# Two attention layers and two feed-forward layers: the order of three engines inside the attention steps

## The chip, the cores and the metric

The kernel runs on one core of a Trainium2 chip. The metric is the time of one execution on the device in microseconds (us). Three runs of the kernel before took 850.15, 852.05 and 856.15 us, so the median is 852.05 us.

The core's engines run side by side, each through its own list of instructions in order, and wait for each other at semaphores: TensorE (PE: matmuls and transposes), VectorE (DVE), ScalarE (ACT), GpSimd (POOL) and SyncE (SP), whose queue issues the transfers.

## The reference, cut to what matters

```python
x = x + xattn0(layernorm(x), ctx, mask, ...)     # x 4 x 1024 x 256, ctx 4 x 77 x 256, 16 heads of 16
x = x + experts(layernorm(x), ...)               # 6 experts, 2 chosen per row
x = x + xattn1(layernorm(x), ctx, ctx, ...)      # one key and one value head for all 16 query heads
x = x + ffn(layernorm(x), ...)                   # 256 -> 1024 -> 256, quantized piecewise-linear gelu

# either attention layer:
scores = einsum('bhnd,bhtd->bhnt', q, k) * scale (+ mask)
attn = softmax(scores, axis=-1)
out = einsum('bhnt,bhtd->bhnd', attn, v)         # then the output projection and the residual
```

The change is in the two attention layers. Everything is computed in float32 accuracy: an operand is split into a leading part and a rest, and three matmuls take the place of one.

## The kernel before, in words

The 4096 rows of x are cut into 8 blocks of 512. Each attention layer (0: steps G = 0 to 7, 1: steps G = 8 to 15) is a software pipeline with one step per block. In step G the kernel works on four blocks at once: scores and weighing of block G; queries and maxima of the next block n = G + 1; the output projection and residual of the one before, p = G - 1; the layer norm of block nm = G + 2. Names of the pieces, with their lines:

- `queries` (L141): 6 matmuls for each half c of the 256 query features, into bank W[c]. ScalarE copies the bank out as qh (`leading`), VectorE subtracts for ql (`rest`, L320 in layer 0, L323 in layer 1).
- `max_unit` (L377, in layer 0 also L380 with the mask): 16 units per block. Each multiplies 128 rows of qh by the keys of 4 heads into one of the two banks X, and VectorE's `take_maxima` (L333) reduces the bank to row maxima mx. Unit u waits until unit u - 2 has been reduced, since there are two banks.
- `turn_maxima` (L386): 4 transposes of mx, then a copy on ScalarE (L301), then a transfer from mt into the stacked query tile qst (L261). The maxima enter the scores as extra rows of the matmul's operand, so no score of the next step can start before this transfer has landed.
- `score` (L402, in layer 0 also L405 with the mask): 16 heads per step, three banks in turn; ScalarE's `exp` (L307) empties them into pt.
- `weigh` (L413): after 4 heads, a quarter, the values are weighed by the exponentials into bank U. Column 16 of each group of 32 holds the sum of the exponentials.
- `divide` (L341, L344, L346): VectorE transposes U into ut, takes the reciprocal of the sums and multiplies. `fold` (L352) transposes two finished quarters back. ScalarE (`lead_quotient`, L312) and GpSimd (`rest_quotient`, L283) make the parts oh and ol.
- `output` (L427, in layer 0 also L422 for the bias): waits for all oh and ol of block p, writes bank W[k]. `add` (L358) adds the bank to x. W[k] is then free for `norm.turn` (L127), which transposes the normed block nm; `norm.lead` and `norm.rest` (L132, L136) split it for the next step's queries.

The order on each engine is written out by hand in loops over G, with the heads i (TensorE) or h (ScalarE) as the clock: `if i in (5, 9, 13): att.weigh(...)` means that this quarter is weighed right after score i. VectorE has no such clock, its calls simply follow each other. The last quarter of block p is weighed at i = 1 of the next step.

In the texts below the layers' steps are told from one score 0 to the next score 0. Quarter 3 of p is `weigh(p, 3)`. "Units" are `max_unit`, "reductions" are L333.

## Time and profile before

| | |
|---|---|
| median of three runs | 852.05 us |
| the profiled execution | 849.2 us |
| its span | 847.4 us |
| busy TensorE / VectorE | 90% / 79% of the span |
| busy ScalarE / GpSimd | 62% / 45% |
| layer 0, score 0 of G = 1 to score 0 of G = 7 | 65.4 to 223.2 us |
| layer 1, score 0 of G = 9 to score 0 of G = 15 | 467.25 to 610.3 us |

The span is what the trace covers, the execution's own time is 1.8 us more. A busy share says how much of the span an engine had work in flight. A TensorE instruction is booked from its issue to its modelled end and overlaps the next one, so start-to-start distances tell what it costs. "Granted clock" is TensorE's clock as a share of 2.4 GHz. The experts (249 to 443 us) and the last feed-forward layer (628 us on) are untouched.

### The profile page before, as it was taken

The numbers are of one execution on the slowest core, as the hardware profiler recorded it, in microseconds if no ns is written. First come the engines' busy times: TensorE is split into PE (matmuls) and PEld (weight loads), VectorE is DVE, ScalarE is ACT, GpSimd is POOL, SyncE is SP. The second block draws the span as 40 slices with busy tenths as digits, with TensorE's granted clock in tenths as the row PEclk, the third lists the DMA queues.
The fourth block names the chain that finished last, engine by engine and source line by source line (L and its number), as shares of the span: only waits on it lengthen the run. The fifth ranks groups of instructions, "written<-read, shape, count | busy, mean of one in ns | idle before, by whom it ended". The sixth has DMA issues, their size and how long they took to land.

```text
span 847.4 us, 13594 instructions
## 1 busy us (share of the span) xinstructions
PE 758.7 (90%) x4388; PEld 556.8 (66%) x4388; DVE 671.9 (79%) x1590; ACT 521.9 (62%) x943; POOL 377.9 (45%) x309
## 2 busy tenths in 40 slices
PE   4799999999899999999989888899888999999995
PEld 3456566665458787877764544455456888889895
DVE  7657777777857777777786888887859899999885
ACT  3455555555644446554436576666667888888884
POOL 5533322223213434344413232122137888988985
PEclk9999999999999999999987999999999999999999
DMA  7965633455100000001066555644400000000001
GB/s 221 157 171 112 141 72 67 97 110 103 46 28 1 1 1 7 2 1 51 1 86 92 76 77 67 115 63 56 58 0 2 2 26 26 26 12 15 26 26 50
DMA packets 24957, 48.51 MB, mean 57 GB/s; under 512 B 3670, under 2 KB 6871, under 8 KB 24376
## 3 DMA queue, kind: packets, MB, share of 16 engines
q1 hardware_dynamic: 23366, 46.54, 28.7%
q10 hardware_dynamic: 1522, 1.11, 0.4%
q8 instruction: 36, 0.59, 0.3%
q14 instruction: 33, 0.27, 0.1%
HBM read 11.99 MB, written 4.19 MB: 19 GB/s over the span
## 4 chain that ended last, share of the span: by engine, by line
PE 54%; DVE 19%; POOL 8%; issue 7%; ACT 6%; DMA 6%; ACTq 0%; DVEq 0%; POOLq 0%
PE bank L141 15%; PE bank L402 6%; PE bank L377 5%; PE bank L427 5%; PE bank L635 5%; DMA qst<-mt 5%; PE bank L413 4%; DVE mx L333 4%; POOL eex L514 4%; PE bank L799 4%; PE bank L405 2%; DVE fpart L754 2%; PE bank L127 2%; POOL frise L706 2%; DVE x L603 2%
## 5 line engine op out<-in xcount | busy, mean ns | idle before, releaser
L307 ACT ACTIVATE pt<-bank 77x512 f32<-77x512 f32 x256 | 146.5, 589 | 122.8 <-PE bank L405 76.3
L333 DVE TENSOR_REDUCE mx<-bank 128x4 f32<-128x308 f32 x256 | 108.9, 471 | 30.5 <-PE bank L380 17.8
L402 PE MATMUL bank<-qst,l_kst 128*77 128x512 f32 (+1 forms) x256 | 107.5, 433 | 19.9 <-DMA qst<-mt 13.9
L706 POOL TENSOR_TENSOR frise<-fg,fg 128x512 f32<-128x512 f32 x64 | 99.2, 1550 | 13.4 <-ACT fg L724 8.9
L377 PE MATMUL bank<-l_kblk,qh 128*128 128x308 f32 x256 | 90.2, 370 | 11.6 <-DVE mx L333 9.4
L402 PEld LDWEIGHTS bank<-qst,l_kst 128*77 128x77 f32 (+1 forms) x256 | 37.0, 149 | 84.2 <-issue 47.9
L103 POOL TENSOR_TENSOR rstd<-var,minus_half 128x4 f32<-128x4 f32 x32 | 34.4, 1074 | 121.1 <-DVE var L98 67.4
L377 PEld LDWEIGHTS bank<-l_kblk,qh 128*128 128x128 f32 x256 | 50.0, 196 | 55.3 <-issue 45.9
L283 POOL TENSOR_TENSOR ol<-ot,oh 128x512 fp32r<-128x512 f32 x32 | 43.1, 1348 | 93.4 <-ACT oh L312 61.3
L603 DVE SCALAR_TENSOR_TENSOR x<-bank,eweight,x 128x256 f32<-128x256 f32 x192 | 79.5, 476 | 4.4 <-PE bank L635 4.1
L799 PE MATMUL bank<-fw2h,fyh 128*128 128x256 f32 x256 | 72.3, 282 | 3.8 <-DVE fyl L766 3.8
L114 ACT ACTIVATE xn<-x,shift,rstd 128x256 f32<-128x256 f32 (+1 forms) x128 | 67.4, 589 | 10.8 <-POOL shift L105 10.8
L713 POOL TENSOR_TENSOR fy<-fpart,fg 128x512 f32<-128x512 f32 x48 | 67.6, 1408 | 13.5 <-DVE fpart L754 10.2
L413 PE MATMUL bank<-pt,l_vall 128*32 128x512 f32 x512 | 69.4, 614 | 4.6 <-DVE ut L341 2.0
L799 PE MATMUL bank<-fw2l,fyh 128*128 128x256 f32 x256 | 72.1, 282 | 0.0
L799 PE MATMUL bank<-fw2h,fyl 128*128 128x256 f32 x256 | 71.9, 281 | 0.0
L754 DVE SCALAR_TENSOR_TENSOR fpart<-ffixed,frise 128x512 f32<-128x512 uint16 x64 | 61.8, 966 | 9.2 <-POOL frise L706 9.2
L635 PE MATMUL bank<-ew2h,ehh 128*128 128x256 f32 x192 | 56.6, 295 | 10.3 <-DVE x L603 10.3
L635 PE MATMUL bank<-ew2l,ehh 128*128 128x256 f32 x192 | 54.6, 285 | 0.0
L635 PE MATMUL bank<-ew2h,ehl 128*128 128x256 f32 x192 | 54.5, 284 | 0.0
L522 ACT ACTIVATE eh<-bank 128x512 f32<-128x512 f32 x48 | 28.7, 597 | 39.7 <-PE bank L141 38.6
L799 PEld LDWEIGHTS bank<-fw2h,fyh 128*128 128x128 f32 x256 | 48.3, 189 | 7.2 <-DVE fyl L766 4.8
(178 smaller groups left out, 2127.9 us busy)
## 6 DMA issues: line engine op xcount, KB each, us to landing
qst<-qh SPq DMA_DIRECT2D x64, 256.0 KB, 6.8
qst<-ql SPq DMA_DIRECT2D x32, 256.0 KB, 9.4
out<-x SPq DMA_DIRECT2D x8, 512.0 KB, 2.6
qst<-ml SPq DMA_DIRECT2D x8, 480.0 KB
x<-in_x SPq DMA_DIRECT2D x3, 1024.0 KB, 12.7
weights<-in_mlp_w SPq DMA_DIRECT2D x2, 1024.0 KB, 5.0
mraw<-in_mask SPq DMA_DIRECT2D x8, 154.0 KB
x<-in_x SPq DMA_DIRECT2D x2, 512.0 KB, 5.9
```

What stands on the lines that cost most here:

```text
L141: last = self.nc.tensor.matmul(out, w, a, start=(first and k == 0), stop=(k == len(ops) - 1))
L307: self.nc.scalar.activation(self.pt[0:T, i // 4 % 2, i % 4, :], self.bank_of(G, i)[0:T, :], ACT.Exp).then_inc(self.probs, 1)
L333: self.nc.vector.reduce_max(out, banks[u % len(banks)][:, 0:4 * T].rearrange("q (p par t) -> q p par t", p=2, par=2), AX.X).then_inc(self. ...
L377: last = self.nc.tensor.matmul(bank, self.qh[:, c, tile], keys, start=True, stop=not layer.masked)
L402: last = self.nc.tensor.matmul(out, layer.kst[rows, layer.stack(c * HC + 2 * k + par), b * T:(b + 1) * T], self.qst[rows, self.slot(G), c ...
L413: last = self.nc.tensor.matmul(self.U[32 * k:32 * k + 32, :], layer.vall[:, self.batch(G), layer.value(c * HC + 2 * k + par), :], self.pt[ ...
L603: last = self.nc.vector.scalar_tensor_tensor(tile, part, self.weight[:, g % 2, 2 * k + t, e:e + 1], tile, ALU.mult, ALU.add)
L635: last = self.nc.tensor.matmul(self.OUT[k][:, t * D:(t + 1) * D], a[:, e % self.R, tile], w[:, e, :], start=(j == 0), stop=(j == 2))
L706: self.nc.gpsimd.tensor_tensor(self.rise[:, k % 2, :], self.g1[:, k % self.R, :], self.g0[:, k % self.R, :], ALU.subtract).then_inc(self.r ...
L713: self.nc.gpsimd.tensor_tensor(self.y[:, k % 2, :], self.part[:, k % 2, :], self.g0[:, k % self.R, :], ALU.add).then_inc(self.y_ready[0], 1)
L754: self.nc.vector.scalar_tensor_tensor(self.part[:, k % 2, :], self.fractions[:, k % self.R, :, 0], 2.0 ** -16, self.rise[:, k % 2, :], ALU ...
L799: last = nc.tensor.matmul(self.OUT[2 * (g % 2) + t // 2][:, t % 2 * D:(t % 2 + 1) * D], a[:, k % self.R, t * P:(t + 1) * P], w[:, c, :], s ...
```

## The change

It does four things, all within the attention steps.

1. `divide` is taken apart. `unfold` (the transpose of U, still once per quarter) stands alone; the new `divide` takes the reciprocals and the quotients of two quarters in one instruction each (tile rden has 32 numbers per partition, not 16).
2. On VectorE the parts of block p's last quarter no longer stand in one run behind four reductions, but singly between pairs of reductions. In layer 1 the first two reductions come ahead of the second `rest`.
3. On TensorE units, queries, weighing and outputs are put at other heads. Both outputs now follow score 10.
4. On ScalarE `lead_quotient` of the first half comes one head earlier, and in layer 1 both `norm.lead` stand together after head 12.

The diff, cut to its core (of layer 0's VectorE loop, which is rearranged like layer 1's, only the different part is shown):

```diff
+    def unfold(self, dve, G, q):
+        dve.wait_ge(self.weighed, 4 * G + q + 1)
+        self.nc.vector.transpose(self.ut[:, q % 2, :], self.U[:, :]).then_inc(self.unfolded, 1)
+
+    def divide(self, dve, G, c):
         nc = self.nc
-        c, par = divmod(q, 2)
-        k = 4 * G + q
-        dve.wait_ge(self.weighed, k + 1)
-        nc.vector.transpose(self.ut[:, q % 2, :], self.U[:, :]).then_inc(self.unfolded, 1)
-        dve.wait_ge(self.unfolded, k + 1)
-        group = self.ut[:, q % 2, :].rearrange("p (j d) -> p j d", d=32)
-        nc.vector.reciprocal(self.rden[:, q % 2, :, :], group[:, :, DH:DH + 1]).then_inc(self.inverse_ready, 1)
-        dve.wait_ge(self.inverse_ready, k + 1)
-        nc.vector.tensor_tensor(self.o32[:, c, :, par, :], group[:, :, 0:DH],
-                                self.rden[:, q % 2, :, :].to_broadcast([P, N // 32, DH]), ALU.mult).then_inc(self.divided, 1)
+        dve.wait_ge(self.unfolded, 4 * G + 2 * c + 2)
+        group = self.ut[:].rearrange("p k (j d) -> p k j d", d=32)
+        nc.vector.reciprocal(self.rden[:], group[:, :, :, DH:DH + 1]).then_inc(self.inverse_ready, 1)
+        dve.wait_ge(self.inverse_ready, C * G + c + 1)
+        nc.vector.tensor_tensor(self.o32[:, c, :, :, :].rearrange("p j k d -> p k j d"), group[:, :, :, 0:DH],
+                                self.rden[:].to_broadcast([P, 2, N // 32, DH]), ALU.mult).then_inc(self.divided, 1)
...
+        UNITS1 = {1: (0,), 2: (1,), 3: (2,), 4: (3,), 5: (4, 5), 6: (6, 7), 7: (8, 9), 9: (10,), 10: (11,), 11: (14, 15)}
...
-                        if h == 3 and p >= BLOCKS:
+                        if h == 2 and p >= BLOCKS:
                             att.lead_quotient(act, p, 0)
...
@@ VectorE, layer 0 (outputs and units 12 to 15)
-                    if p >= 0:
-                        for k in range(2):
-                            att.add(dve, p, k)
+                    if p >= 0:
+                        att.add(dve, p, 0)
                     if n < BLOCKS:
                         att.take_maxima(dve, n, range(12, 16), att.X)
+                    if p >= 0:
+                        att.add(dve, p, 1)
...
@@ VectorE, layer 1
                     if n < 2 * BLOCKS:
-                        for c in range(C):
-                            att.rest(dve, n, c)
-                        att.take_maxima(dve, n, range(0, 4), att.X)
+                        att.rest(dve, n, 0)
+                        att.take_maxima(dve, n, range(0, 2), att.X)
+                        att.rest(dve, n, 1)
                     if p >= BLOCKS:
-                        att.divide(dve, p, 3)
+                        att.unfold(dve, p, 3)
+                    if n < 2 * BLOCKS:
+                        att.take_maxima(dve, n, range(2, 4), att.X)
+                    if p >= BLOCKS:
+                        att.divide(dve, p, 1)
+                    if n < 2 * BLOCKS:
+                        att.take_maxima(dve, n, range(4, 6), att.X)
+                    if p >= BLOCKS:
                         att.fold(dve, p, 1)
                     if n < 2 * BLOCKS:
-                        att.take_maxima(dve, n, range(4, 10), att.X)
-                    att.divide(dve, G, 0)
+                        att.take_maxima(dve, n, range(6, 10), att.X)
+                    att.unfold(dve, G, 0)
                     if n < 2 * BLOCKS:
-                        att.take_maxima(dve, n, range(10, 12), att.X)
+                        att.take_maxima(dve, n, range(10, 14), att.X)
                     if p >= BLOCKS:
-                        for k in range(2):
+                        for k in range(C):
                             att.add(dve, p, k)
                     if n < 2 * BLOCKS:
-                        att.take_maxima(dve, n, range(12, 16), att.X)
+                        att.take_maxima(dve, n, range(14, 16), att.X)
...
-                    att.divide(dve, G, 1)
+                    att.unfold(dve, G, 1)
+                    att.divide(dve, G, 0)
                     att.fold(dve, G, 0)
...
-                    att.divide(dve, G, 2)
+                    att.unfold(dve, G, 2)
...
@@ TensorE, layer 0
-                        if 3 <= i <= 10 and n < BLOCKS:
...
-                        if i in (5, 9, 13):
-                            att.weigh(pe, l0, G, i // 4 - 1)
...
+                        if i in (2, 4, 7, 9) and n < BLOCKS:
+                            for u in {2: (0, 1), 4: (2, 3), 7: (8, 9), 9: (10, 11)}[i]:
                                 att.max_unit(pe, l0, n, u, att.X)
+                        if i == 6:
...
+                                for u in (4, 5):
+                                    att.max_unit(pe, l0, n, u, att.X)
+                            att.weigh(pe, l0, G, 0)
+                            if n < BLOCKS:
+                                for u in (6, 7):
+                                    att.max_unit(pe, l0, n, u, att.X)
+                        if i == 10:
+                            for k in range(C):
...
+                                    att.output(pe, l0, p, k)
+                                if n < BLOCKS:
+                                    for u in (12 + 2 * k, 13 + 2 * k):
+                                        att.max_unit(pe, l0, n, u, att.X)
+                            att.weigh(pe, l0, G, 1)
+                        if i == 12:
+                            if n < BLOCKS:
+                                att.turn_maxima(pe, n, att.X[0])
+                            for c in range(C):
...
+                                    norm.turn(pe, nm, c, att.W[c])
+                        if i == 15:
+                            att.weigh(pe, l0, G, 2)
...
@@ TensorE, layer 1
-                        if i < C and n < 2 * BLOCKS:
-                            att.queries(pe, l1, n, i)
-                        if i == 1 and p >= BLOCKS:
+                        if i == 1 and n < 2 * BLOCKS:
+                            for c in range(C):
+                                att.queries(pe, l1, n, c)
+                        if i == 5:
+                            att.weigh(pe, l1, G, 0)
+                        if i in UNITS1 and n < 2 * BLOCKS:
+                            for u in UNITS1[i]:
+                                att.max_unit(pe, l1, n, u, att.X)
+                        if i == 2 and p >= BLOCKS:
                             att.weigh(pe, l1, p, 3)
...
+                        if i == 10:
+                            for k in range(C):
...
+                                    att.output(pe, l1, p, k)
+                                if k == 0 and n < 2 * BLOCKS:
+                                    for u in (12, 13):
+                                        att.max_unit(pe, l1, n, u, att.X)
+                        if i == 11:
+                            att.weigh(pe, l1, G, 1)
...
-                        if i in (11, 12) and nm <= LN_FFN:
+                        if i in (12, 13) and nm <= LN_FFN:
...
+                        if i == 14:
+                            att.weigh(pe, l1, G, 2)
```

How the instructions then stand, at three places of layer 1's step G = 11. First VectorE, from the rest of the queries to the additions of block p. Before:

```order
L323 TENSOR_TENSOR ql<-bank,qh 128x512 x2
L333 TENSOR_REDUCE mx<-bank 128x2x2 x4
L341 STREAM_TRANSPOSE ut<-bank 128x512
L344 RECIPROCAL rden<-ut 128x16
L346 TENSOR_TENSOR o_67<-ut,rden 128x16x16
L352 STREAM_TRANSPOSE ot<-o_67 128x512
L333 TENSOR_REDUCE mx<-bank 128x2x2 x6
L341 STREAM_TRANSPOSE ut<-bank 128x512
L344 RECIPROCAL rden<-ut 128x16
L346 TENSOR_TENSOR o_67<-ut,rden 128x16x16
L333 TENSOR_REDUCE mx<-bank 128x2x2 x2
L358 TENSOR_TENSOR x<-x,bank 128x512 x2
```

With the change:

```order
L323 TENSOR_TENSOR ql<-bank,qh 128x512
L333 TENSOR_REDUCE mx<-bank 128x2x2 x2
L323 TENSOR_TENSOR ql<-bank,qh 128x512
L338 STREAM_TRANSPOSE ut<-bank 128x512
L333 TENSOR_REDUCE mx<-bank 128x2x2 x2
L344 RECIPROCAL rden<-ut 128x32
L346 TENSOR_TENSOR o_67<-ut,rden 128x2x16x16
L333 TENSOR_REDUCE mx<-bank 128x2x2 x2
L352 STREAM_TRANSPOSE ot<-o_67 128x512
L333 TENSOR_REDUCE mx<-bank 128x2x2 x4
L338 STREAM_TRANSPOSE ut<-bank 128x512
L333 TENSOR_REDUCE mx<-bank 128x2x2 x4
```

The run of four VectorE instructions (L341 to L352) between reductions 4 and 5 is gone: one transpose (now L338), one joined reciprocal, one joined multiplication and the fold each have reductions around them, and reductions 12 and 13 stand ahead of the additions.

Second TensorE, from the quarter 3 of block p to the first score after `weigh(G, 0)`; L413 is `weigh`, L377 a unit. Before:

```order
L413 MATMUL bank<-pt,l_vall 32x512 x4
L402 MATMUL bank<-qst,l_kst 77x512 x2
L377 MATMUL bank<-l_kblk,qh 128x308 x2
L402 MATMUL bank<-qst,l_kst 77x512
L377 MATMUL bank<-l_kblk,qh 128x308 x2
L402 MATMUL bank<-qst,l_kst 77x512
L377 MATMUL bank<-l_kblk,qh 128x308 x2
L413 MATMUL bank<-pt,l_vall 32x512 x4
L402 MATMUL bank<-qst,l_kst 77x512
```

With the change:

```order
L377 MATMUL bank<-l_kblk,qh 128x308
L402 MATMUL bank<-qst,l_kst 77x512
L377 MATMUL bank<-l_kblk,qh 128x308
L413 MATMUL bank<-pt,l_vall 32x512 x4
L402 MATMUL bank<-qst,l_kst 77x512
L377 MATMUL bank<-l_kblk,qh 128x308
L402 MATMUL bank<-qst,l_kst 77x512
L377 MATMUL bank<-l_kblk,qh 128x308
L402 MATMUL bank<-qst,l_kst 77x512
L413 MATMUL bank<-pt,l_vall 32x512 x4
L377 MATMUL bank<-l_kblk,qh 128x308 x2
L402 MATMUL bank<-qst,l_kst 77x512
```

Unit 0 and unit 1 now stand ahead of `weigh(p, 3)`, and units are one per score up to unit 3.

Third TensorE, from `weigh(G, 1)` to the end of the step; L386 turns the maxima, L127 is `norm.turn`. Before:

```order
L413 MATMUL bank<-pt,l_vall 32x512 x4
L402 MATMUL bank<-qst,l_kst 77x512
L377 MATMUL bank<-l_kblk,qh 128x308 x2
L402 MATMUL bank<-qst,l_kst 77x512
L127 MATMUL bank<-ident,xn 128x128 x4
L402 MATMUL bank<-qst,l_kst 77x512
L386 MATMUL bank<-ident,mx 16x128 x4
L127 MATMUL bank<-ident,xn 128x128 x4
L402 MATMUL bank<-qst,l_kst 77x512
L413 MATMUL bank<-pt,l_vall 32x512 x4
L402 MATMUL bank<-qst,l_kst 77x512 x3
```

With the change:

```order
L377 MATMUL bank<-l_kblk,qh 128x308 x2
L413 MATMUL bank<-pt,l_vall 32x512 x4
L402 MATMUL bank<-qst,l_kst 77x512
L386 MATMUL bank<-ident,mx 16x128 x4
L127 MATMUL bank<-ident,xn 128x128 x4
L402 MATMUL bank<-qst,l_kst 77x512
L127 MATMUL bank<-ident,xn 128x128 x4
L402 MATMUL bank<-qst,l_kst 77x512
L413 MATMUL bank<-pt,l_vall 32x512 x4
L402 MATMUL bank<-qst,l_kst 77x512 x3
```

The first `norm.turn` has moved from ahead of the turned maxima to behind them, the last two units from behind `weigh(G, 1)` to ahead of it, and `weigh(G, 2)` by one score towards the step's end. In layer 0 the same transposes move in the same direction, and `weigh(G, 2)` is the last thing of the step.

## Rows read from the trace of the kernel before

**Rows 1.** Windows, one step each: us, busy us per engine (instructions), granted clock, DMA.

```profile
144.30:170.60 26.30, 25.32 (x146) 16.30 (x146) 19.69 (x48) 14.77 (x27) 7.13 (x8) 1.00 0.44 91
444.50:467.20 22.70, 19.61 (x80) 10.34 (x80) 15.56 (x41) 13.92 (x26) 6.90 (x5) 0.77 0.60 93
467.20:491.70 24.50, 22.07 (x112) 13.23 (x112) 19.94 (x48) 15.90 (x30) 5.07 (x5) 0.93 0.50 67
515.90:539.10 23.20, 20.83 (x113) 11.76 (x113) 19.29 (x50) 14.93 (x29) 5.12 (x5) 1.00 0.58 81
562.40:587.00 24.60, 22.08 (x112) 13.21 (x112) 20.06 (x48) 15.55 (x30) 6.41 (x7) 0.93 0.50 66
```

**Rows 2.** Chain of waits, a step of layer 0: start us, us, what.

```profile
144.32 0.46 PE bank L402
...
170.60 0.46 PE bank L402
```

**Rows 3.** Timeline of TensorE, same step: start us, us, instruction, idle before.

```profile
158.09 0.38 PE L377 MATMUL bank<-l_kblk,qh 128*128 128x308 f32 x1
...
164.69 0.31 PE L377 MATMUL bank<-l_kblk,qh 128*128 128x308 f32 x1
...
166.33 0.60 PE L386 MATMUL bank<-ident,mx 128*16 128x128 f32 x4
```

**Rows 4.** Chain of waits, a step of layer 1.

```profile
515.87 0.46 PE bank L402
516.33 1.39 PE bank L141 x6
...
519.34 0.99 PE bank L413 x8
...
528.51 1.44 PE bank L427 x12
...
536.14 2.90 DMA qst<-mt
...
539.08 0.46 PE bank L402
```

**Rows 5.** Timeline of TensorE, same step of layer 1.

```profile
520.79 0.45 PE L377 MATMUL bank<-l_kblk,qh 128*128 128x308 f32 x2
...
534.85 0.60 PE L386 MATMUL bank<-ident,mx 128*16 128x128 f32 x4
```

**Rows 6.** Timeline of VectorE, same step of layer 1.

```profile
516.33 1.40 DVE L90 BATCH_NORM_STATS2 stats<-x 128x6 f32<-128x256 f32 x4
...
520.00 0.69 DVE L323 TENSOR_TENSOR ql<-bank,qh 128x512 fp32r<-128x512 f32 x1 [0.92 <-ACT qh L296]
521.13 0.87 DVE L333 TENSOR_REDUCE mx<-bank 128x4 f32<-128x308 f32 x2 [0.44 <-PE bank L377]
...
524.44 0.71 DVE L352 STREAM_TRANSPOSE ot<-o 128x512 f32<-128x512 f32 x1
...
532.12 0.69 DVE L358 TENSOR_TENSOR x<-x,bank 128x512 f32<-128x512 f32 x1 [1.39 <-PE bank L427]
```

**Rows 7.** Instructions on tile rden, all steps: duration ns min/median/max, first and last start.

```profile
L344 DVE RECIPROCAL rden<-ut x64: 252/253/255, 55.6 to 629.9; 128x16 f32<-128x16 f32 x64
L346 DVE TENSOR_TENSOR o<-ut,rden x64: 424/425/1481, 55.9 to 630.1; 128x256 f32<-128x256 f32 x64
```

**Rows 8.** Groups of VectorE by form: busy us, mean ns, idle before us.

```profile
L136 DVE TENSOR_TENSOR xl<-bank,xh 128x512 fp32r<-128x512 f32 x32 | 21.5, 683 | 10.7 <-ACT xh L132 10.7
...
L584 DVE RECIPROCAL ertotal<-etotal 128x4 f32<-128x4 f32 x8 | 1.4, 178 | 0.3
```

**Rows 9.** Timeline of GpSimd, same step of layer 1.

```profile
525.95 1.28 POOL L283 TENSOR_TENSOR ol<-ot,oh 128x512 fp32r<-128x512 f32 x1 [2.19 <-issue]
```

**Rows 10.** Timeline of TensorE, last step of layer 0.

```profile
232.67 0.47 PE L422 MATMUL bank<-bias,ones 128*128 128x512 f32 x1 [2.76 <-POOL ol L283]
```

**Rows 11.** Timeline of GpSimd, end of a step of layer 0.

```profile
168.22 1.29 POOL L273 TENSOR_TENSOR ml<-mraw,mh 77x512 fp32r<-77x512 f32 x1
```

94 lines of the change are left out of this document (47 added, 47 removed).

## The prediction

> **What bounds the kernel now.** I read three views in this order. The windows, cut at the first score of a step, show that a step of layer 0 lasts 26.3 us with TensorE booked for 25.3 of them, and a step of layer 1 lasts 23.2 us with TensorE booked for 20.8 and VectorE for 19.3 [rows 1]. Neither engine is full in layer 1, so a chain through several must set its length. The chain of waits shows which: it comes back to the transfer of the turned maxima before each first score, 144.32 to 170.60 in layer 0 [rows 2] and 515.87 to 539.08 in layer 1, where the transfer alone takes 2.90 us [rows 4]. So a step has two pieces. From its score 0 to the turned maxima (TM) it takes 166.33 - 144.32 = 22.0 us in layer 0 [rows 2, 3] and 534.85 - 515.87 = 19.0 us in layer 1 [rows 4, 5]. From TM to the next score 0 it takes 4.3 us in layer 0 [rows 2, 3] and 4.2 in layer 1 [rows 4, 5]: transposes, copy, transfer. The change cannot shorten the second piece, only fill it. The timelines show what fills the first. In layer 0 it is TensorE, with stalls too small to be listed as idle: a unit's matmul that waits for its bank is booked at 0.38 us, a free one at 0.31 [rows 3]. In layer 1 it is a queue on VectorE: 16 reductions from 521.13 on, with the division, the fold and the additions between them [rows 6].
>
> **Layer 1, step by step.** First piece, until the first reduction. Before, it starts 5.26 us after score 0: both halves of the queries, `weigh(p, 3)` and two more scores are ahead of unit 0 on TensorE, and on VectorE the second `rest` at 520.00, itself 0.92 late, is ahead of the reduction [rows 6]. Afterwards unit 0 has ahead of it two scores (0.53 us, estimated from the 0.46 of the first and the spacing behind it) and two halves of 1.39 [rows 4], so it starts at 3.3; it reached its reduction 0.34 after its start (520.79 to 521.13 [rows 5, 6]), 0.44 with the first fill. The first reduction then starts at 3.75, **1.5 us earlier**.
>
> Second, from the first reduction to TM. VectorE's items now: 16 reductions of 0.435 (a pair books 0.87 [rows 6]), 7.0; `rest` 0.62; two transposes at 0.71 [rows 6], 1.4; one joined division; fold 0.7; two additions, 1.3. The joined division has no row. The multiplication of 256 numbers takes 0.425 [rows 7], one of 512 by the nearest row 0.683 [rows 8]. The reciprocal takes 0.178 for 4 numbers [rows 8] and 0.253 for 16 [rows 7], so by the same slope 0.35 for 32. Together 1.05 with gaps, where two single ones cost 1.4: **0.35 us saved per pair**, bounded by 0 and 0.68 (nothing gained, or one of the two free); I take the nearest rows. The items sum to 12.1 us. I add 0.8 for a unit's way there and back (one each time VectorE catches up with TensorE). The piece ends 12.9 us behind the first reduction; before it was 534.85 - 521.13 = 13.7. **0.8 us less.** What makes it shorter though it holds more: before, VectorE stood 1.39 us for the second output ahead of its last four reductions [rows 6], and TensorE stood while VectorE ran four instructions in a row.
>
> Third, TensorE has two `norm.turn` behind TM (four transposes are booked 0.60 [rows 3], 0.44 without the overlap of some 0.16), three scores of 0.24 and a weighing of 0.99 [rows 4]: 2.6 us of work in 4.2, hidden. VectorE has behind its last reduction an unfold, joined division, fold, two `norm.rest` and an unfold, in all 4.4 us, and then the statistics, 2.1 us from their row to the next `rest` [rows 6]; that `rest` can't start before qh is there, some 2.7 us into the step, so about 0.5 us of slack are left. The step is then 20.9 us, 2.3 less. I take 2.0, since the walk has no queueing noise in it; bounds are 0.4 (only the division's saving arrives) and 2.6 (the 0.8 vanish too). Six full steps, G = 9 to 14: **12.0 us** (2.4 to 15.6).
>
> The Trainium skill (VectorE: DVE Perf Modes, "The TRN2 errata") gives an SBUF-to-SBUF instruction a fixed part of 58 cycles, 0.06 us. By it a joined division would save 0.12 us and not 0.35, and six steps 1.4 us less. The trace disagrees: a reciprocal of 4 numbers takes 0.178 us [rows 8], so the fixed part is over twice that.
>
> **TensorE's clock.** Of the steps of layer 1, one at full granted clock (2.4 GHz) lasts 23.2 us, two at 0.93 last 24.5 and 24.6 [rows 1]. Part of such a step runs at 1.2 GHz, for 1.2 to 1.4 us. With less waiting per step I count one of the two gone: **1.2 us** (2.4 more lost to 2.4 gained).
>
> **First step of layer 1, G = 8.** It has no block p, lasts 22.7 us and has the lowest clock, 0.77 [rows 1]. Units and reductions are denser here too, and no unit waits for an output. I take **2.2 us**, as in a full step; bounds 0 and 4.0, the latter if the low clock goes as well.
>
> **Layer 0.** TensorE's own work up to TM: 13 scores with mask, 0.23 for each of two matmuls, 6.1; queries 2.8; three weighings of 0.99 with gaps of some 0.17, 3.5; 16 units of two matmuls, each booked 0.31 [rows 3] less the overlap of 0.16, 4.8; two outputs of 1.44 [rows 4] with a bias of 0.23, 3.3; one `norm.turn` 0.44. That is 20.9 of the 22.0 us, so 1.1 are stalls. The `norm.turn` moves behind TM: 0.44 gone for certain. Of the stalls the new spacing (two units per one or two scores, the division between pairs) removes some; I take half of the 1.1, so **1.0 us** a step, bounds 0.44 and 1.55. Seven steps, G = 0 to 6: **7.0 us** (3.1 to 10.9).
>
> **The last steps.** In G = 7 output 0 stood 2.76 us for GpSimd [rows 10]. Two more scores, 0.9 us, now stand ahead of it and fill that; behind, the weighings wait less for the exponentials. **1.3 us** (0 to 2). But `weigh(7, 2)` and `weigh(7, 3)` now stand back to back with an unfold of 0.71 between, which is counted in. In G = 15 two scores likewise, against a joined division on the way to the last output: **0.3 us** (-0.5 to 0.8).
>
> **Sum.** 12.0 + 1.2 + 2.2 + 7.0 + 1.3 + 0.3 = 24.0 us. The profiled execution took 849.2 us and would take 825.2. The median shown is 852.05, 2.85 above it, so I forecast **828.0 us** for the median. All low bounds together leave a gain of 2.6, all high ones 35.7.
>
> **Rivals.**
> - *The wait for the outputs comes back at another place.* In layer 1 the last two reductions stand behind both additions. The outputs now follow score 10, with the parts of p made later: fold, oh, ol. Before, ol ended at 525.95 + 1.28 = 527.2 [rows 9], 1.1 us before output 0 began; in my walk it ends 0.15 before. If VectorE's 1.4 us before the addition [rows 6] returns, six steps lose 8.4 and layer 0 half of its 7.0: 828 + 8.4 + 3.5 = 840 us. For it: that thin margin. Against it: TensorE gets to the outputs with units ahead that VectorE must have served.
> - *The clock falls in every step of layer 1.* The lowest granted clock stands in the step without outputs [rows 1], where units alternate with waits; the new order spreads units further. Six falls for two at 1.3 us: 828 + 1.2 + 5.2 = 834 us.
>  The Trainium skill (TensorE: Matmul & The Clock Gate, "HAM oscillation") has short idle stretches between groups of matmuls take the clock down and up again; by it each new gap costs, and the time would be these 834 us.
> - *GpSimd holds the division up.* The multiplication reads and writes SBUF only; its longest of 64 took 1.48 us where 0.425 is the median [rows 7]. In layer 0 the joined one stands just where GpSimd does mask instructions without a pause between, 1.29 us for one of them [rows 11]. Held until two have ended, with 1 us of slack: 1.6 us in seven steps, 11 us: 839 us.
>  The Trainium skill (SBUF — State Buffer, "Who interferes with whom") makes this an exclusive lock for the whole instruction when VectorE has two SBUF inputs; by it the wait is whole and not shared.
> - *Slower.* The chain fold, oh, ol, output, addition decides each step: output 0 comes late by more than 2.3 us in layer 1 and 1.4 in layer 0, because exponentials behind a late oh on ScalarE hold back scores and so TensorE. Each us beyond that costs 13 steps 13 us; 1 us gives 865. Against it: ol took 1.28 us [rows 9], and three banks let two scores run ahead of ScalarE.
> - *The joined instructions don't save.* The division's rows bound this at 4 us: 832.
>
> **Chances.** Forecast with its sizes (816 to 837) 0.66; wait comes back 0.14; clock 0.07; GpSimd 0.04; joined instructions 0.04; slower 0.05. The range for 8 in 10 goes from 817 to 843. A change under 1% (8.5 us) can't be told from none by a measurement of this kernel. Of the cases, the first rival half lands within 1%, as does a little of the forecast: faster 0.84, within 1% 0.11, slower 0.05.
>
> **What would show it.** Score 0 to score 0: about 25.3 us in layer 0 and 21.2 in layer 1. First reduction of layer 1 about 3.8 us after score 0. VectorE's wait before L358 nearly gone. L346 32 times at 0.69, L344 at 0.35. First score's wait for the transfer under 1 us in layer 0, still 1 to 1.5 in layer 1. Wrong, if VectorE waits before the additions or TensorE before the outputs in full steps, if L346 means over 0.9, or if the clock in layer 1's windows is below 0.93 in most.

## The result, and the profile after

The changed kernel takes **816.17 us** (median of four runs, 810.88 to 822.52) against 851.1 for the kernel before (four runs, 847.85 to 856.15). The ratio is 0.960, 95% interval 0.955 to 0.965: 4% faster. The forecast was 828.0 with a range of 817 to 843; the median lies 0.8 us under its lower end. The profiled execution took 817.71 us with a span of 815.9, 31.5 less than the 847.4 of before. The terms are compared against these 31.5 us; the medians lie 34.9 us apart, since the profiled execution of before is 1.9 us under its median and this one 1.5 over.

First the windows, one step each, to set beside [rows 1]: length, busy time (instructions) of TensorE's matmuls, its weight loads, VectorE, ScalarE and GpSimd, granted clock, DMA share, GB/s. The first is a step of layer 0, the second is G = 8, the others are two steps of layer 1.

```profile
139.91:164.71 24.80, 24.30 (x146) 16.50 (x146) 18.74 (x44) 14.33 (x27) 7.32 (x8) 1.00 0.48 97
...
431.59:449.78 18.19, 16.22 (x80) 8.49 (x81) 15.43 (x39) 14.24 (x26) 6.91 (x5) 1.00 0.74 113
...
511.35:531.96 20.61, 19.07 (x112) 11.61 (x112) 19.06 (x46) 14.90 (x29) 5.27 (x6) 1.00 0.69 118
531.96:552.49 20.53, 18.95 (x113) 11.71 (x113) 18.10 (x45) 15.09 (x30) 6.43 (x7) 1.00 0.60 80
```

A step of layer 0 went from 26.3 to 24.8 us, one of layer 1 from 23.2 to 24.6 down to 20.5, and G = 8 from 22.7 at a clock of 0.77 to 18.2 at 1.00. Next the chain of waits in the step of layer 1 from 511.35 on (start, us, what), beside [rows 4].

```profile
511.39 0.69 PE bank L402 x2
512.08 2.88 PE bank L141 x12
...
515.14 0.86 DVE mx L333 x2
...
519.85 0.62 DVE ot L352
...
522.78 1.57 PE bank L427 x12
...
524.64 1.42 PE bank L427 x12
...
529.09 2.87 DMA qst<-mt
531.96 0.04 issue
532.00 0.68 PE bank L402 x2
```

The first half of the step now belongs to VectorE, the second to TensorE with its two outputs. The timeline of VectorE in the same step, beside [rows 6]; the bracket is idle time before the row and what ended it.

```profile
515.14 0.86 DVE L333 TENSOR_REDUCE mx<-bank 128x4 f32<-128x308 f32 x2
515.92 0.68 DVE L323 TENSOR_TENSOR ql<-bank,qh 128x512 fp32r<-128x512 f32 x1
...
524.54 0.86 DVE L333 TENSOR_REDUCE mx<-bank 128x4 f32<-128x308 f32 x2 [0.91 <-PE bank L377]
525.32 1.47 DVE L358 TENSOR_TENSOR x<-x,bank 128x512 f32<-128x512 f32 x2
```

The 1.39 us ahead of the second addition are gone; 0.91 us now stand ahead of reductions 12 and 13. The first reduction starts at 515.14, where before it came 5.26 us into the step. TensorE's first output and the turned maxima of this step, and GpSimd's ol that the output needs, beside [rows 5, 9]:

```profile
522.70 0.35 PE L427 MATMUL bank<-l_woh,oh 128*128 128x256 f32 x1
...
527.79 0.60 PE L386 MATMUL bank<-ident,mx 128*16 128x128 f32 x4
```

```profile
521.26 1.29 POOL L283 TENSOR_TENSOR ol<-ot,oh 128x512 fp32r<-128x512 f32 x1 [3.25 <-issue]
```

ol ends at 522.55, the output begins at 522.70. The two instructions on tile rden in all steps (ns min/median/max, first and last start), beside [rows 7]:

```profile
L344 DVE RECIPROCAL rden<-ut x32: 330/353/355, 60.0 to 591.8; 128x32 f32<-128x32 f32 x32
L346 DVE TENSOR_TENSOR o<-ut,rden x32: 691/692/694, 60.4 to 592.2; 128x512 f32<-128x512 f32 x32
```

Where the 31.5 us came from, by score 0 of each step:

| stretch | forecast | measured |
|---|---|---|
| layer 0 up to score 0 of G = 7 | 7.0 | 8.9 |
| G = 7 and the experts | 1.3 | 4.1 |
| G = 8 | 2.2 | 4.5 |
| six steps G = 9 to 14, at full clock | 12.0 | 17.8 |
| the clock in these six | 1.2 | 2.1 |
| G = 15 and the last feed-forward layer | 0.3 | -5.9 |

For the fourth and fifth row: before, the six steps took 24.51, 24.11, 23.21, 23.43, 24.55 and 23.26 us. The first and the fifth hold a fall of the clock (0.93). The other four ran at 1.00 and mean 23.50, and 6 x (23.50 - 20.53) = 17.8; what the two had above 23.50, 2.1, is put down to the clock. The second, 24.11, is long for another reason: one multiplication of its division took 1.29 us where 0.425 is the median, and it stands on the chain of waits. GpSimd was at work when it began (the kernel before):

```profile
504.52 1.32 POOL L1075 TENSOR_TENSOR fw1l<-weights,fw1h 128x512 fp32r<-128x512 f32 x1 [1.40 <-ACT fw1h L1229]
```

```profile
504.83 1.29 DVE L346 TENSOR_TENSOR o<-ut,rden 128x256 f32<-128x256 f32 x1
```

The last row is a loss that nobody forecast. In the last feed-forward layer, whose code is unchanged, the clock fell four times. Windows of 2 us of the changed kernel around one of them:

```profile
670.00:672.00 2.00, 0.26 (x3) 0.05 (x1) 2.00 (x3) 1.97 (x5) 1.84 (x3) 1.00 0.20 80
672.00:674.00 2.00, 1.90 (x9) 1.65 (x10) 1.05 (x2) 1.97 (x5) 1.92 (x2) 0.84 0.45 182
674.00:676.00 2.00, 2.00 (x10) 1.83 (x9) 1.26 (x2) 1.40 (x3) 1.92 (x2) 0.50 0.00 0
676.00:678.00 2.00, 2.00 (x11) 1.84 (x11) 2.00 (x4) 1.14 (x3) 1.32 (x2) 0.81 0.00 0
```

TensorE idled from 670 to 672, worked again, and then ran at 0.50 (1.2 GHz) through a whole window: 0.16 x 2 + 0.50 x 2 + 0.19 x 2 = 1.7 us lost. The gap is a wait for ScalarE's normalized rows; the kernel before has it too, and no fall behind it. One row from the timeline of the changed kernel, then one from that of before, then two windows of before around it:

```profile
672.10 0.66 PE L127 MATMUL bank<-ident,xn 128*128 128x128 f32 x4 [1.85 <-ACT xn L114]
```

```profile
709.77 0.66 PE L127 MATMUL bank<-ident,xn 128*128 128x128 f32 x4 [1.88 <-ACT xn L114]
```

```profile
708.00:710.00 2.00, 0.23 (x2) 0.23 (x3) 2.00 (x3) 1.97 (x5) 1.92 (x2) 1.00 0.36 147
710.00:712.00 2.00, 2.00 (x13) 1.75 (x12) 0.86 (x3) 1.97 (x5) 1.92 (x2) 1.00 0.29 115
```

### The profile page after: what moved, and what is told of

Its sections match the earlier page's. It is cut to its first block, busy times and chain, and to the rows that moved or that the text cites. A ratio compares the mean times of both kernels' runs of the same rounds, so it can differ in the third digit from the quotient of the medians.

```text
span 815.9 us, 13530 instructions
## 1 busy us (share of the span) xinstructions
PE 739.3 (91%) x4388; PEld 556.8 (68%) x4388; DVE 655.0 (80%) x1526; ACT 515.4 (63%) x943; POOL 376.7 (46%) x309
## 3 DMA queue, kind: packets, MB, share of 16 engines
q1 hardware_dynamic: 23366, 46.54, 29.7%
## 4 chain that ended last, share of the span: by engine, by line
PE 52%; DVE 19%; POOL 8%; issue 7%; ACT 6%; DMA 6%; DVEq 0%; ACTq 0%; POOLq 0%
PE bank L141 16%; PE bank L635 6%; PE bank L427 5%; PE bank L402 5%; DMA qst<-mt 5%; PE bank L377 4%; PE bank L413 4%; POOL eex L514 4%; DVE mx L333 3%; PE bank L405 3%; PE bank L799 3%; DVE fpart L754 2%; POOL frise L706 2%; PE bank L380 2%; DVE x L603 2%
## 5 line engine op out<-in xcount | busy, mean ns | idle before, releaser
L307 ACT ACTIVATE pt<-bank 77x512 f32<-77x512 f32 x256 | 140.6, 588 | 85.3 <-PE bank L405 62.7
L333 DVE TENSOR_REDUCE mx<-bank 128x4 f32<-128x308 f32 x256 | 108.9, 470 | 24.4 <-PE bank L380 13.7
L402 PE MATMUL bank<-qst,l_kst 128*77 128x512 f32 (+1 forms) x256 | 103.0, 417 | 16.4 <-DMA qst<-mt 10.7
L706 POOL TENSOR_TENSOR frise<-fg,fg 128x512 f32<-128x512 f32 x64 | 97.0, 1516 | 18.4 <-ACT fg L724 13.9
L377 PE MATMUL bank<-l_kblk,qh 128*128 128x308 f32 x256 | 81.5, 336 | 9.8 <-DVE mx L333 6.0
L283 POOL TENSOR_TENSOR ol<-ot,oh 128x512 fp32r<-128x512 f32 x32 | 41.3, 1292 | 97.2 <-ACT oh L312 53.7
L402 PEld LDWEIGHTS bank<-qst,l_kst 128*77 128x77 f32 (+1 forms) x256 | 36.6, 146 | 65.7 <-ACT pt L307 24.8
L799 PE MATMUL bank<-fw2h,fyh 128*128 128x256 f32 x256 | 74.1, 289 | 3.8 <-DVE fyl L766 3.8
L377 PEld LDWEIGHTS bank<-l_kblk,qh 128*128 128x128 f32 x256 | 48.0, 192 | 43.2 <-issue 34.0
L413 PE MATMUL bank<-pt,l_vall 128*32 128x512 f32 x512 | 68.2, 604 | 2.0 <-ACT pt L307 1.0
L799 PEld LDWEIGHTS bank<-fw2h,fyh 128*128 128x128 f32 x256 | 50.3, 196 | 7.4 <-DVE fyl L766 4.8
L748 DVE TENSOR_SCALAR ffixed<-bank 128x512 int32<-128x512 f32 x64 | 43.5, 680 | 13.9 <-PE bank L141 13.6
```

Of the source, the lines that this page charges most:

```text
L307: self.nc.scalar.activation(self.pt[0:T, i // 4 % 2, i % 4, :], self.bank_of(G, i)[0:T, :], ACT.Exp).then_inc(self.probs, 1)
L333: self.nc.vector.reduce_max(out, banks[u % len(banks)][:, 0:4 * T].rearrange("q (p par t) -> q p par t", p=2, par=2), AX.X).then_inc(self. ...
L377: last = self.nc.tensor.matmul(bank, self.qh[:, c, tile], keys, start=True, stop=not layer.masked)
L402: last = self.nc.tensor.matmul(out, layer.kst[rows, layer.stack(c * HC + 2 * k + par), b * T:(b + 1) * T], self.qst[rows, self.slot(G), c ...
L413: last = self.nc.tensor.matmul(self.U[32 * k:32 * k + 32, :], layer.vall[:, self.batch(G), layer.value(c * HC + 2 * k + par), :], self.pt[ ...
L706: self.nc.gpsimd.tensor_tensor(self.rise[:, k % 2, :], self.g1[:, k % self.R, :], self.g0[:, k % self.R, :], ALU.subtract).then_inc(self.r ...
```

## The experiments

**The same kernel again.** No edit: are the four falls the change's?

> The changed kernel once more, nothing edited. It tells how far one profile can be trusted. First theory: the first 573 us repeat (a step of layer 0 24.8 us, of layer 1 20.5), and the 6 us that the changed kernel lost behind the attention layers, where the granted clock stood at 0.94 in four stretches of 30 us, do not belong to the change: the falls come and go from run to run. Then this profile shows another number of falls in the last feed-forward layer, and the time varies by up to 6 us with it. Rival: the falls come from where that layer now starts behind the shortened steps; then there are four again. Time expected: 810 to 822 us.

817.2 us (812.43 to 820.93, four runs; ratio 0.963, 0.960 to 0.966), span 810.6. The steps are the same: 24.8 us in layer 0, 20.5 in layer 1. In the last feed-forward layer, TensorE's waits and one of the windows (the three behind it, up to 768 us, also show 1.00):

```profile
PE bank L127 <- ACT xn L114: 10.3, 6, 1.9
```

```profile
648.00:678.00 30.00, 28.15 (x180) 25.27 (x180) 27.86 (x50) 26.93 (x49) 25.99 (x20) 1.00 0.08 32
```

The same six gaps, one of 1.2 us and five of 1.8 to 1.9, and no fall behind them. One fall stands just ahead of this layer, at 596 to 600 us, behind a wait of 1.88 us for ol; the first profile has that wait too, without a fall. So the falls vary from run to run of one kernel. The times go with the mean clock: the four runs took 812.43, 816.69, 817.72 and 820.93 us at mean granted clocks of 0.986, 0.982, 0.980 and 0.976. At equal clock the change keeps its gain, though its size is not sharp: before took 846.72 and 847.65 us at 0.986, 34 to 35 us above 812.43; 849.34 at 0.980, 32 above 817.72; 849.67 and 851.67 at 0.976, 29 to 31 above 820.93.

**The gap closed.** In the last feed-forward layer the turn of the next rows comes one part later on TensorE, ScalarE and VectorE:

```diff
-                    if c in (4 if g == 0 else 2, 6) and g + 1 < BLOCKS:
+                    if c in (4 if g == 0 else 3, 6) and g + 1 < BLOCKS:
...
-                    if c in (5 if g == 0 else 3, 7) and g + 1 < BLOCKS:
+                    if c in (5 if g == 0 else 4, 7) and g + 1 < BLOCKS:
...
-                    if c == (3 if g == 0 else 1) and g + 1 < BLOCKS:
+                    if c == (3 if g == 0 else 2) and g + 1 < BLOCKS:
```

> The changed kernel with one more edit: in the last feed-forward layer the first transposes of the next block, its copy and its rest each come one part later (part 2, 3, 4, not 1, 2, 3). There TensorE stood 1.85 us for ScalarE's normed rows, five times, and behind four of these gaps the clock fell. First theory: the gap is what lets the clock fall; without it there are no falls in that layer, and the gaps themselves are gone if nothing else limits: up to 5 x 1.85 = 9 us and 6 us of clock, 801 to 812 us. Rival: that layer is bound by GpSimd, VectorE and ScalarE together (each 83 to 97% busy), so TensorE's gap only moves to another place: then the time stays at 810 to 818 us, with falls or without.

810.73 us (810.66 to 811.07), ratio 0.954 (0.953 to 0.956), faster than both kernels. TensorE's waits in the same stretch:

```profile
PE bank L799 <- DVE fyl L766: 3.4, 3, 1.7
PE bank L127 <- ACT xn L114: 2.4, 5, 0.6
PE bank L141 <- DVE fxl L136: 2.4, 5, 1.0
```

8 us of waiting are gone, 5 came in at other places. The four runs lie within 0.4 us of each other, at the best value of the changed kernel (810.88, at a clock of 0.988). So closing the gap made the good case hardly shorter, and the four falls of the first profile are not there. One other fall is, of 1.7 us at 606 to 612, behind a wait of 2.70 us at the layer's start that both profiles of the changed kernel have without one. That the closed gap keeps the falls away is not shown: the four kernels below that stand on this one spread by 1.9 to 5.3 us over their runs.

**Only VectorE's order and the joined division** (TensorE and ScalarE as before):

> VectorE's order and the joined divisions of the changed kernel, TensorE's and ScalarE's order of the kernel before. Theory: in layer 1 a step is a queue on VectorE that TensorE has to feed in time; with TensorE's old order unit 0 still stands behind both queries, weigh(p, 3) and two scores, so the first reduction still starts 5.2 us after score 0, and only part of the 0.8 us behind it is won: 0.3 to 1.0 us a step in layer 1, 0 to 0.5 in layer 0, 843 to 849 us for a kernel before of 851. Rival: taking the division apart is the change's whole worth, TensorE's order follows from it: then 820 to 828 us.

845.77 us (840.73 to 853.32, ten runs), ratio 0.996 (0.992 to 1.000). Steps of 25.9 us in layer 0 and 23.65 in layer 1; three of the six of layer 1 hold a fall of the clock, the others took 22.94, 23.00 and 23.43. VectorE now waits for TensorE: its waits for units in layer 1, 470 to 570 us, and in layer 0, 65 to 225 us (us, times, longest), and a row of its timeline:

```profile
DVE mx L333 <- PE bank L377: 19.9, 19, 2.1
```

```profile
DVE mx L333 <- PE bank L380: 26.6, 24, 3.0
```

```profile
508.90 0.87 DVE L333 TENSOR_REDUCE mx<-bank 128x4 f32<-128x308 f32 x2 [2.05 <-PE bank L377]
```

In the kernel before these two sums are 5.2 and 13.7 us. VectorE is ready for the first maxima 2 us before TensorE delivers a unit. Its clock was also low: a mean of 0.958 to 0.984 in the ten runs.

**Only TensorE's and ScalarE's order** (VectorE as before, single divisions):

> TensorE's and ScalarE's order of the changed kernel, VectorE's order and single divisions of the kernel before. Theory: unit 0 comes 1.6 us earlier in layer 1, but VectorE takes it only behind the second rest (about 4.8 us after score 0 and not 3.8), then stands for the second output ahead of four reductions as before, which now comes later (behind score 10): 0 to 1.5 us a step won in layer 1. In layer 0 the transposes behind the turned maxima give 0.4 us a step, and the rest of the 1.5 us is lost: the kernel takes 832 to 848 us, and with dve_order_only the two parts do not add up to the 35 us of the whole. Rival: TensorE's order alone is worth most of it: 820 to 828 us.

851.88 us (849.55 to 856.33, ten runs), ratio 1.003 (1.000 to 1.005). My expectation of a gain was wrong. Steps of 27.2 us in layer 0, longer than the 26.3 of before, and 23.7 in layer 1. Here TensorE waits: in layer 0 from 65 to 225 us, then in layer 1 from 470 to 570.

```profile
PE bank L377 <- DVE mx L333: 12.1, 12, 1.3
```

```profile
PE bank L377 <- DVE mx L333: 6.9, 10, 1.0
PE bank L413 <- DVE ut L341: 4.2, 4, 1.1
```

The first was 1.0 us before. TensorE sends units between the outputs, where VectorE still stands for the output ahead of its last four reductions; two full banks later TensorE stands as well. So the halves of the change are worth 5 us less and 1 us more by themselves, and 34 together.

**The change with single divisions:**

```diff
-        nc.vector.reciprocal(self.rden[:], group[:, :, :, DH:DH + 1])...
+        for par in range(2):
...
+            nc.vector.reciprocal(self.rden[:, par, :, :], group[:, :, DH:DH + 1])...
+            dve.wait_ge(self.inverse_ready, k + 1)
+            nc.vector.tensor_tensor(self.o32[:, c, :, par, :], group[:, :, 0:DH], ...
```

> The change with the joined division taken back: at the place of each joined reciprocal and multiplication stand two single ones (16 reciprocals and 256 products each), everything else as in the changed kernel. Theory (VectorE's first pair lies on the way to the turned maxima in layer 1, layer 0 is TensorE's): single ones cost 2 x (0.25 + 0.425) against 0.35 + 0.69, so about 0.35 us more per pair; seven steps of layer 1 lose 0.35 each, layer 0 nothing: +2 to +3 us against the changed kernel, some 818 to 820 us. Rival 1 (the saving is absorbed where VectorE waits 0.9 us for units between the outputs): no difference, 816 to 817. Rival 2 (it counts in both layers and for both pairs): +5 to +10 us, 822 and more.

819.86 us (817.33 to 822.47), ratio 0.962 (0.957 to 0.967). The interval overlaps that of the change, so the trace has to tell: a step of layer 0 is 24.92 us against 24.78, and one of layer 1 (from one copy of the turned maxima to the next) took 22.05 in G = 9, with a fall of the clock at 460 to 464, and 20.72 on average in the five behind it, against 20.53.

```profile
L346 DVE RECIPROCAL rden<-ut x64: 209/244/252, 59.2 to 594.7; 128x16 f32<-128x16 f32 x64
L348 DVE TENSOR_TENSOR o<-ut,rden x64: 424/425/428, 59.4 to 595.0; 128x256 f32<-128x256 f32 x64
```

By 6 x 0.19 + 7 x 0.14 the joined division brings 2.1 us here (an estimate from these steps); 0.19 per step of layer 1 is about half of the 0.35 forecast for one pair. The forecast time, 818 to 820, was met, but more than 1 us of it is the fall.

**The joined division alone** in the old order, where the second quarter's division stood:

> The kernel before with one thing of the change: the divisions of two quarters joined, at the places where the second quarter's division stood before; orders of TensorE and ScalarE as before, and VectorE's otherwise too. Theory (the joined division is worth its 0.35 us where VectorE sets the turned maxima, layer 1 alone): 2 to 3 us less than before, ratio 0.997. Rival (it carries a large part of the change's gain of 34 us): ratio under 0.985. Rival (a longer block of VectorE between units costs what it saves): ratio 1.000 or over.

852.11 us (847.13 to 856.29, ten runs), ratio 1.002 (0.998 to 1.006): nothing. Layer 1's steps stay at 23.87 us on average (two hold a fall, as before), layer 0's grow from 26.3 to 26.7. One step did get shorter, G = 10, from 24.11 to 23.40: its product is not held here. In layer 0 the run transpose, division, fold lasts 2.5 us without a reduction in it, and VectorE's waits for the outputs rose from 13.3 us to this (layer 0):

```profile
DVE x L358 <- PE bank L427: 17.9, 12, 2.0
```

**Both turns behind the turned maxima, alone:**

```diff
-                        if i in (11, 12) and nm <= BLOCKS:
...
-                            norm.turn(pe, nm, i - 11, att.W[i - 11])
+                        if i == 12 and nm <= BLOCKS:
+                            for c in range(C):
...
+                                norm.turn(pe, nm, c, att.W[c])
```

> The kernel before with one thing of the change: both turns of the normalized block stand behind the turned maxima on TensorE in both layers (one stood ahead), with ScalarE's copies after them. Theory: in layer 0, where TensorE is the piece's bound, 0.44 us per step come off, 3 us in seven steps; in layer 1 the queue on VectorE sets the turned maxima and nothing comes off: ratio 0.9965. Rival (both layers): 6 us, ratio 0.993. Rival (the turns come late for the next step's queries): no gain or a loss, ratio 1.000 or over.

843.38 us (841.63 to 846.72), ratio 0.990 (0.985 to 0.995), more than expected. Layer 0's steps are 25.9 us, 0.4 less: the expected 0.44. Layer 1's are 23.4, all at full clock; the four that ran at full clock before too mean 23.3 against 23.5. At equal clock it is 4 us faster (842.45 at 0.984, where before took 845.96 and 847.38). The rest came with fewer clock falls: none between 444 and 600 us, where the profile of before has four windows of 12 us at 0.73 to 0.90. Whether the order keeps them away is open; its own runs went from 0.978 to 0.988.

**Both rests first**, on the kernel with the gap closed (810.73):

```diff
-                        att.rest(dve, n, 0)
-                        att.take_maxima(dve, n, range(0, 2), att.X)
-                        att.rest(dve, n, 1)
+                        for c in range(C):
+                            att.rest(dve, n, c)
+                        att.take_maxima(dve, n, range(0, 2), att.X)
```

> The changed kernel with the later turn in the second layer's feed-forward part (810.7 us), and in layer 1 both halves of the low query part (the rest) ahead of the first two reductions on VectorE, as before the change, instead of two reductions between them. Theory (VectorE's queue sets the first half of a step of layer 1): the first reduction starts 1.1 us later, after the second copy of qh, but the third only 0.5 later, and 0.4 to 0.5 us of it reach the step: 20.5 becomes 21.0 us, seven steps 3 us, 813.7 us. Rival (TensorE alone sets the step, with VectorE's 0.9 us of waiting for the units between the outputs as cover): 20.5 and 810.7. Rival (the whole 1.1 us reaches the step): 21.6 and 818.

813.95 us (813.78 to 815.69), ratio 0.957 (0.955 to 0.959); a step of layer 1 is 20.9 us. VectorE's timeline:

```profile
518.70 0.69 DVE L323 TENSOR_TENSOR ql<-bank,qh 128x512 fp32r<-128x512 f32 x1 [0.54 <-ACT qh L296]
519.31 0.85 DVE L333 TENSOR_REDUCE mx<-bank 128x4 f32<-128x308 f32 x2
```

The forecast 813.7 holds: the two reductions between the rests fill the wait for the second half of qh, and are worth 3.2 us. In the first half of such a step VectorE is the bound, as the forecast of this run had it.

**Units 14 and 15 ahead of output 1**, same base (VectorE takes their maxima ahead of both additions):

```diff
-        UNITS1 = {..., 9: (10,), 10: (11,), 11: (14, 15)}
+        UNITS1 = {..., 9: (10,), 10: (11,)}
...
-                                    for u in (12, 13):
+                                    for u in (12, 13, 14, 15):
...
-                        att.take_maxima(dve, n, range(10, 14), att.X)
+                        att.take_maxima(dve, n, range(10, 16), att.X)
```

> The same base (810.7 us). In layer 1 TensorE does units 14 and 15 behind 12 and 13, between the two outputs, instead of behind score 11, and VectorE takes their maxima ahead of both additions. Theory: in the changed kernel the end of the step's first piece is output 1, addition 1 (it can only start when output 1 ends), the last two reductions, turned maxima: 525.9 + 0.25 + 0.65 + 0.86 = 527.8 us in the step that began at 511.35. Without the addition on the way TensorE gets to the turned maxima when its own queue does, some 0.4 us earlier: 20.5 becomes 20.1 us, seven steps 3 us, 808 us. Rival (VectorE has only 1.1 us idle in a step, its queue behind the turned maxima sets the next step's first reduction): no gain, 810.7. Rival (additions late for the next norm): slower, 812 and more.

817.94 us (816.63 to 820.04), ratio 0.962 (0.959 to 0.964): 7 us slower than the base; a step of layer 1 takes 21.6 us. **The turned maxima also ahead of the second weighing:**

```diff
-                        if i == 11:
-                            att.weigh(pe, l1, G, 1)
-                        if i == 12 and n < 2 * BLOCKS:
-                            att.turn_maxima(pe, n, att.X[0])
+                        if i == 11:
+                            if n < 2 * BLOCKS:
+                                att.turn_maxima(pe, n, att.X[0])
+                            att.weigh(pe, l1, G, 1)
```

> As the run with units 14 and 15 between the outputs, and the turned maxima ahead of the second weighing on TensorE (0.99 us) instead of behind it, with ScalarE's copy of them behind exponential 11. Theory: up to 1.4 us less to the turned maxima; but VectorE has 19.4 us of work in a step of 20.5 and becomes the bound: 19.6 us a step, seven steps 6 us, 804.5 us. Rival (the transfer of 2.9 us then ends before TensorE's work behind the turned maxima is done, so the step falls only by TensorE's 0.9 us of waiting and its 0.65 for reductions): 19.2 to 19.6. Rival (ScalarE's exponentials hold it): no gain over the run without it.

816.02 us (813.08 to 818.41), ratio 0.958 (0.954 to 0.961); steps of 21.0 us, and 21.9 in the one with a fall of the clock. Both times my theory fell. TensorE's timeline in the second of them, then VectorE's:

```profile
528.17 0.77 PE L377 MATMUL bank<-l_kblk,qh 128*128 128x308 f32 x2 [0.52 <-DVE mx L333]
```

```profile
530.40 0.69 DVE L358 TENSOR_TENSOR x<-x,bank 128x512 f32<-128x512 f32 x1 [0.35 <-PE bank L427]
532.09 0.72 DVE L338 STREAM_TRANSPOSE ut<-bank 128x512 f32<-128x512 f32 x1 [1.01 <-PE bank L413]
```

TensorE stands 0.52 us for a bank between the outputs, which delays output 1 and all behind it, and VectorE stands 1.01 us for the weighing that moved back. Behind that transpose are the division, the fold, two rests and the statistics, which VectorE must finish before the next step's first reduction. With only some 1 us of idle time in a step it can't make up for 1.4 us of standing. Moving the turned maxima forward moved the wait onto the engine that had no room.

**The third weighing of layer 0's last step behind score 13**, same base. In the changed kernel TensorE stands there for a transpose:

```profile
234.02 1.06 PE L413 MATMUL bank<-pt,l_vall 128*32 128x512 f32 x8 [0.93 <-DVE ut L338]
```

```diff
-                        if i == 15:
+                        if i == (15 if n < BLOCKS else 13):
```

> The changed kernel with the later turn of the second layer's feed-forward part (which measured 810.7 us), and in the last step of layer 0's attention the third weighing behind score 13 instead of 15, so that the third and fourth don't stand back to back with VectorE's transpose of 0.7 between (a wait of 0.93 us before the fourth in the changed kernel). Theory: that wait goes, 0.9 us less: 809.8 us. Rival: the wait is only moved, since the last exponentials set the fourth weighing: 810.7 as without it.

812.47 us (811.75 to 814.15), ratio 0.953 (0.949 to 0.957): no gain, rather a loss. The last weighing begins 20.4 us after score 0 of this step, where it was 19.7. The wait is only moved, and there are two of them:

```profile
230.41 1.07 PE L413 MATMUL bank<-pt,l_vall 128*32 128x512 f32 x8 [0.73 <-ACT pt L307]
...
234.61 1.06 PE L413 MATMUL bank<-pt,l_vall 128*32 128x512 f32 x8 [0.68 <-ACT pt L307]
```

Both weighings now wait for exponentials.

## Why the prediction was right, and where its sizes were off

**The mechanism.** The forecast said that the chain through VectorE's queue and the outputs sets the steps of layer 1 and TensorE's own queue those of layer 0, and that interleaving shortens both. It did. What it did not say is that neither engine's order does it alone. The two one-sided kernels show this: 0.996 and 1.003.

**Layer 1, the walk.** Its three pieces came out nearly to the tenth. First reduction after score 0: forecast 3.75, measured 515.14 - 511.39 = 3.75. From there to the turned maxima: 12.9, measured 527.79 - 515.14 = 12.65. From there to score 0: 4.2, measured 532.00 - 527.79 = 4.2. The walk gave 2.3 us for this step, G = 11, and 23.21 - 20.61 = 2.6 was measured; over the four steps at full clock the gain is 3.0. The sizing step that failed is "I take 2.0, since the walk has no queueing noise in it". The new order has less waiting than the old (VectorE's waits from 470 to 570 us fell from 15.0 to 9.2), so the discount took 0.3 us off a number that was already 0.3 low. The walk also took G = 11, the shortest of the six steps, for all of them: G = 10 holds the multiplication of 1.29 us, 0.87 over the median, which the forecast knew from its row [rows 7] only as a risk for the new kernel and not as a cost of the old. Six steps brought 17.8 us, over the upper bound of 15.6.

**The joined division.** Forecast 1.05 us for a pair (0.35 and 0.69), measured 0.353 + 0.692; two single ones took 2 x (0.244 + 0.425) = 1.34. So 0.3 us are saved: from 256 to 512 products the time grows by 0.267 us, which leaves 0.158 fixed. What it is worth to the kernel depends on its place: some 2 us in the new order, nothing in the old. The 58 cycles that the forecast took from the Trainium skill (VectorE: DVE Perf Modes, "The TRN2 errata") are corrected in the same section, which gives (N + 151)/0.96 ns for an fp32 instruction of this kind. By that the two products would take 0.424 and 0.691 us, an estimate from the page; the trace agrees, with 0.425 and 0.692.

**Layer 0.** Forecast 1.0 us a step, measured 1.5. The turn behind the turned maxima brought its 0.4 (0.44 forecast as certain). Of the 1.1 us of stalls I took half. All went: score 0 to the turned maxima is now 160.40 - 139.95 = 20.45 us, and the 20.9 that I had added up as TensorE's own work, less the turn's 0.44, are 20.46. VectorE still waits for outputs there, 9.3 us in six steps against 13.3, but TensorE is booked for 24.3 of 24.8 us, so this costs nothing.

**The clock in layer 1.** Forecast 1.2 us for the six steps and at most 1.8 of G = 8. Measured 2.1, and some 2.6 of the 4.5 in G = 8: without the falls of that profile the old order does that step in 21.6 us (between two copies of the turned maxima, in the run with only the turns moved), the new in 19.85, which is 1.7 by order. The rival in which the clock falls in every step did not come: all windows of layer 1 show 1.00. The falls of the last feed-forward layer stand each behind a gap of 1.84 to 1.90 us. But a fifth gap, of 1.79, has none behind it, and in another run the same gaps have none at all, so a gap alone does not decide it. The rule of short idle stretches that the forecast names stands in the Trainium skill (TensorE: Matmul & The Clock Gate) not under "HAM oscillation" but under "A second HAM failure mode: psum-queue depth-cycling": frequent short idle stretches between groups of matmuls take the clock down and up. The trace agrees only in part, by the four falls and the fifth gap without one.

**G = 7 and the experts.** Forecast 1.3, measured 4.1. From the last copy of turned maxima in layer 0 to the first in layer 1 before took 219.9 us, the changed kernel 215.7, and three kernels with the old order of TensorE there (only VectorE's order, only the joined division, only the turns) 216.8 to 216.9. So the order brings 1.2 us, as forecast. The kernel with only TensorE's and ScalarE's order has the same 215.7. The other 3.0 belong to the one execution that I read. Its clock is 0.74 from 234 to 240 us, 1.6 us lost, and its wait for GpSimd [rows 10] is 2.76 us where the other three have 1.2, as here in the kernel with the turns alone:

```profile
228.68 0.47 PE L422 MATMUL bank<-bias,ones 128*128 128x512 f32 x1 [1.19 <-POOL ol L283]
```

**The last feed-forward layer.** Forecast 0.3 with G = 15, measured -5.9: four falls behind gaps that both kernels have. Falls there come and go between runs. The parts that hang on single executions nearly cancel: 3.0 in G = 7, 2.6 and 2.1 by the clock of layer 1, and these -5.9. That they do is luck. What is left of the 31.5, about 29.7 us, compares with 24.0 - 1.2 = 22.8 in the forecast, so the order was worth some 7 us more than I had worked out.

**The rivals.** The wait for the outputs was the likeliest, with a margin of 0.15 us between ol and output 0; the trace shows just that, 522.55 to 522.70, and no wait. GpSimd did not hold the division in the changed kernel: all 32 joined products took 691 to 694 ns. But the mechanism is real. In the changed kernel a joined product of layer 0 begins in five steps just before GpSimd's mask instruction, and that one takes 1.15 to 1.18 us instead of 1.04:

```profile
135.99 0.69 DVE L346 TENSOR_TENSOR o<-ut,rden 128x512 f32<-128x512 f32 x1
```

```profile
136.42 1.16 POOL L269 TENSOR_TENSOR mh<-mraw,zero 77x512 fp32r<-77x512 f32 x1 [8.12 <-PE bank L386]
```

In the kernel with only VectorE's order GpSimd begins first, and five joined products of layer 0 took 1.29 to 1.31 us:

```profile
139.13 1.04 POOL L269 TENSOR_TENSOR mh<-mraw,zero 77x512 fp32r<-77x512 f32 x1 [8.89 <-PE bank L386]
```

```profile
139.42 1.30 DVE L346 TENSOR_TENSOR o<-ut,rden 128x512 f32<-128x512 f32 x1
```

Each costs VectorE 0.6 us; the forecast had put 1.6 us a step on it. Which of the two begins first was not worked out there, so that it went well was luck. The slower case did not come, but it can be made: units 14 and 15 ahead of output 1 put back 1 us a step.

## What to carry to other kernels

Where two engines feed each other through a few banks, their orders are one decision: change one alone and the wait goes to the other; count the gain only for the pair. Walk one step instruction by instruction with measured durations and trust the sum, once the step is seen to be like its neighbours; look then at which engine has no idle time left, since it can't make up for a wait moved onto it. Before a time of one profile is called the change's, look at the granted clock in that stretch in a second run.

## What the hardware showed

Behind four of five gaps of TensorE of 1.8 to 1.9 us the granted clock went to 0.50 in one run, which cost 1.7 us each time; in another run of the same kernel the same gaps cost nothing. The mean clock of a run and its time go together: 812.43 us at 0.986, 820.93 at 0.976. With that gap cut to 0.6 us the four runs agreed within 0.4 us, but kernels built on that one spread by up to 5.3 us.

A VectorE product that began while GpSimd worked on an instruction with 512 numbers per partition waited: 1.29 us where 0.425 is usual (256 numbers), 1.30 where 0.692 is usual (512). It ended 0.28 and 0.55 us after GpSimd's instruction. A product that began first was not held, and GpSimd's instruction took 1.16 us instead of 1.04.

A VectorE product of 512 numbers per partition took 0.692 us where 256 took 0.425, and a reciprocal of 32 took 0.353 where 16 took 0.244 to 0.253: joining two saves about 0.15 us each.
